# An attention layer and a quantised feed-forward layer on one core: chunk work re-timed, queries seven steps ahead, down projection in six banks

## What is computed

```python
def xattn(query, key, value, mask, Wq, Wk, Wv, Wo):       # 8 x 128 tokens of 512; 32 query heads, 8 kv heads of 128
    q, k, v = heads(query @ Wq), heads(key @ Wk), heads(value @ Wv)
    q, k = apply_rope(q), apply_rope(k)
    logits = einsum('btkgd,bTkd->bkgtT', q, k) * 0.0884
    logits = where(mask, 30 * tanh(logits / 30), -1e30)
    return einsum('bkgtT,bTkd->btkgd', softmax(logits), v) @ Wo

def ffn(x, w1, w2, w3):                                     # 512 -> 1376 -> 512
    dq1, dq2, dq3 = (nf4_quant_dequant(w) for w in (w1, w2, w3))
    return (silu(x @ dq1.T) * (x @ dq2.T)) @ dq3.T

def nf4_quant_dequant(w):                                   # blocks of 64 values
    absmax = max(abs(block)); n = block / absmax
    return NF4_CODE[searchsorted(bounds, n)] * absmax       # 15 bounds, 16 codes

x = x + xattn(layernorm(x), ctx, ctx, mask, ...)
x = x + ffn(layernorm(x), w1, w2, w3)
```

## Time and profile before

| | us |
|---|---|
| median of 3 runs | 882.83 |
| lowest and highest | 882.04, 887.17 |
| the profiled execution, its time | 888.34 |
| its span, first to last instruction | 886.5 |
| PE busy | 815.5 (92%) |
| DVE busy | 684.7 (77%) |
| POOL busy | 484.2 (55%) |
| ACT busy | 464.8 (52%) |

### The profile page before, as it was taken

The page is one execution under the profiler, slowest core; times in us unless marked ns, Lnnn a source line. Parts: engine busy times, 40 slices in busy tenths (PEclk is TensorE's granted clock), DMA queues, the critical chain, the costliest instruction groups (busy, mean ns, idle before and its releaser), DMA issues.

```text
span 886.5 us, 10685 instructions
## 1 busy us (share of the span) xinstructions
PE 815.5 (92%) x3806; PEld 647.4 (73%) x3806; DVE 684.7 (77%) x745; ACT 464.8 (52%) x571; POOL 484.2 (55%) x270
## 2 busy tenths in 40 slices
PE   6798998899899899998999999989779999996898
PEld 4577886688677677776778777767567788885786
DVE  3886853887988789897989989968789889985220
ACT  5025842664766566637647656544544658576100
POOL 2555055675977669769879779683212134432100
PEclk9999999999999999999999999989989999998899
DMA  9667556233343433433434424214003113111210
GB/s 318 187 189 202 167 137 199 72 84 84 109 111 85 135 84 96 126 85 81 139 83 112 132 66 154 72 36 131 30 1 126 36 48 113 48 56 37 74 60 36
DMA packets 63541, 91.76 MB, mean 104 GB/s; under 512 B 6784, under 2 KB 30464, under 8 KB 63488
## 3 DMA queue, kind: packets, MB, share of 16 engines
q1 hardware_dynamic: 62304, 88.25, 34.5%
q10 hardware_dynamic: 1184, 2.82, 0.9%
HBM read 51.00 MB, written 19.07 MB: 79 GB/s over the span
## 4 chain that ended last, share of the span: by engine, by line
PE 54%; DVE 20%; POOL 10%; issue 7%; DMA 5%; ACT 3%; SPq 1%; DVEq 0%; POOLq 0%; ACTq 0%
PE bank L473 5%; PE bank L475 5%; PE bank L474 5%; POOL qT L1169 4%; PE bank L507 4%; PE bank L509 4%; PE bank L508 4%; PE bank L553 3%; PE avp L581 3%; DVE nfv L908 3%; PE bank L493 3%; PE bank L491 3%; PE bank L492 3%; PE trp L480 3%; DVE nfx L908 3%
## 5 line engine op out<-in xcount | busy, mean ns | idle before, releaser
L1226 POOL TENSOR_TENSOR eb<-eb,maskf 128x512 f32<-128x512 f32 x64 | 106.7, 1667 | 53.8 <-ACT eb L782 53.7
L780 ACT ACTIVATE eb<-bank 128x512 f32<-128x512 f32 x64 | 38.1, 595 | 155.8 <-PE bank L553 155.8
L1169 POOL TENSOR_TENSOR qT<-cs_loop,sw 128x512 f32<-128x512 f32 x58 | 90.7, 1564 | 49.2 <-DMA sw<-cs_loop 47.2
L507 PE MATMUL bank<-woh,ath 128*128 128x512 f32 x256 | 110.0, 430 | 0.0
L491 PE MATMUL bank<-xh,wqh 128*128 128x512 f32 x256 | 106.4, 416 | 0.0
L509 PE MATMUL bank<-woh,atl 128*128 128x512 f32 x256 | 103.1, 403 | 0.0
L508 PE MATMUL bank<-wol,ath 128*128 128x512 f32 x256 | 103.0, 402 | 0.0
L493 PE MATMUL bank<-xh,wql 128*128 128x512 f32 x256 | 101.3, 396 | 0.0
L492 PE MATMUL bank<-xl,wqh 128*128 128x512 f32 x256 | 101.1, 395 | 0.0
L716 ACT ACTIVATE nfq<-nfv,bnd 128x1408 uint8<-128x1408 f32 x60 | 84.9, 1461 | 19.7 <-POOL nfv L1185 19.7
L908 DVE SCALAR_TENSOR_TENSOR nfa<-nfq,nfa 128x1408 f32<-128x1408 uint8 x42 | 88.4, 2104 | 0.8
(11 more groups left out here) (140 smaller groups left out, 1960.9 us busy)
## 6 DMA issues: line engine op xcount, KB each, us to landing
sw<-cs_loop SPq DMA_DIRECT2D x116, 128.0 KB, 2.3
stage<-wq_pieces SPq DMA_DIRECT2D x32, 256.0 KB, 2.9
stage<-wo_pieces SPq DMA_DIRECT2D x32, 256.0 KB, 3.0
stage<-dq_scratch SPq DMA_DIRECT2D x32, 256.0 KB, 3.7
sw<-cs_start SPq DMA_DIRECT2D x44, 128.0 KB, 2.4
ks_scratch<-qT SPq DMA_DIRECT2D x16, 256.0 KB, 2.5
vs_scratch<-vst SPq DMA_DIRECT2D x16, 256.0 KB, 2.6
kcur<-ks_scratch SPq DMA_DIRECT2D x16, 256.0 KB, 2.9
```

What stands on the lines that cost most here:

```text
L507: nc.tensor.matmul(o, ah, wh[:, g, :], start=g == 0, stop=False)
L1169: nc.gpsimd.tensor_tensor(dst, products(ru, slot)[:, 0, :], sw[:, slot, :], ALU.add).then_inc(roped, 1)
L1226: nc.gpsimd.tensor_tensor(part, part, maskf[:, :].rearrange("p (o t) -> p o t", o=1).to_broadcast([128, G, S]), ALU.mult).then_inc(weights ...
```

## The change

Query units run seven steps ahead instead of six; the first seven are done in the start phase, and weight pieces are split one step earlier, `high(32)` and `low(32)` ahead of the loop. In the loop every step has exactly two places of NF4 work; the next chunk's maximum stands behind ten additions of the chunk (before: twelve), in the step's own order. POOL divides at the head of the step after that. The loop's last four steps have none of it; the hidden layer has 50 places in 22 units (before: 44), the down projection's first five tiles have 9 additions, behind `w3l` in each tile (before: 3, in two tiles, ahead of it). The chunks of w1 and w2 come in turn, so that the hidden layer starts after fewer of them. Masks of chunks 9 to 11 have a ring of five buffers of their own (`nfz`). The down projection adds up six sequences at a time, two follow.

```diff
-        AHEAD = 6
+        AHEAD = 7
...
-            return {8: 0, 10: 1, 12: 2, 13: 3, 14: 4, 15: 5}.get(v)
+            return {7: 0, 9: 1, 11: 2, 12: 3, 13: 4, 14: 5, 15: 6}.get(v)
...
         def nf_before(slot):
-            if slot <= 56:
-                return max(0, slot - 2) * 116 // 54
             if slot <= NSTEP:
-                return 116 + (0, 1, 2, 3, 4, 6, 8, 10, 12)[slot - 56]
-            return min(128 + 2 * (slot - NSTEP), 16 * 11)
+                return 2 * min(max(0, slot - 2), 58)
+            if slot <= NSTEP + 2 * HT:
+                return 116 + 50 * (slot - NSTEP) // (2 * HT)
+            return min(166 + 2 * (slot - NSTEP - 2 * HT), 16 * 11)
...
-            return [(1 + p // 16, p % 16 - p % 16 // 13) for p in at if p % 16 != 12]
+            return [(1 + p // 16, p % 16 - p % 16 // 11) for p in at if p % 16 != 10]
...
-            return [c for c in range(2, 12) if nf_before(slot) <= 16 * c - 20 < nf_before(slot + 1)]
+            return [c for c in range(2, 12) if nf_before(slot) <= 16 * c - 22 < nf_before(slot + 1)]
...
 SP, in a step of the loop
-                    head_piece(j + 3)
+                    head_piece(j + 4)
...
-                    for c in nf_finished(j - 2):
+                    for c in nf_finished(j - 1):
                         nf_store(c)
-                    for c in nf_finished(j - 3):
+                    for c in nf_finished(j - 2):
...
                     if last and b == 3:
-                        sp.wait_ge(nf_out, nf_stored(NKV - 1))
+                        sp.wait_ge(nf_out, nf_stored(2))
...
 PE, down projection
-            outs = [prj[0], prj[1], prj2[0], prj2[1]]
+            outs = [prj[0][:, :], prj[1][:, :], prj2[0][:, :], prj2[1][:, :], avp[:, 0, :], avp[:, 1, :]]
...
-                for b in range(4):
-                    last = down(b, n, outs[b][:, :])
+                for b in range(6):
+                    last = down(b, n, outs[b])
...
-            for b in range(4, B):
-                pe.wait_ge(final_done, b - 3)
+            for b in range(6, B):
+                pe.wait_ge(final_done, b - 5)
...
 ACT
-                    if not last:
-                        high(32 + j)
+                    if j + 1 < 8 * NKV - 8:
+                        high(33 + j)
...
             weights(0)
+            high(32)
             weights(1)
...
 DVE, down projection
-                if 1 <= n < 3:
-                    for c, i in nf_adds(NSTEP + 2 * HT + n - 1):
-                        nf_add(c, i)
                 nc.vector.tensor_tensor(w3l[0:p, n, :].rearrange("h (a r q) -> h a q r", a=2, q=2),
...
+                for c, i in nf_adds(NSTEP + 2 * HT + n):
+                    nf_add(c, i)
...
 POOL
             for u in range(AHEAD):
-                if u == 5:
+                if u == AHEAD - 1:
                     mask(0)
                 query_rope(u)
...
             mask(1)
+            nf_normalise(1)
+            weight_low(32)
...
+                    for c in nf_prepares(j - 1):
+                        nf_normalise(c)
                     for c in nf_finished(j - 1):
                         nf_rescale(c)
...
                     if j + AHEAD < NUNIT:
                         query_rope(j + AHEAD)
-                    for c in nf_prepares(j) if j else (1,):
-                        nf_normalise(c)
...
-            nf_rescale(NKV)
```

More of the change, by code:

```diff
@@ L132, in build @@
             cs_start = sb("cs_start", [128, 2, 2, 512], f32, start)
+        with ExitStack() as ffn:
+            nfz = sb("nfz", [128, 5, CH], u8, ffn)
         wol1 = sb("wol1", [128, G, D], f32r)
@@ L434, in _ @@
             sp.dma_start(vcur[:, 4:8, 0:DH], vs_d[0, 1]).then_inc(v_in[1], 16)
-            for p in range(3):
+            for p in range(4):
                 head_piece(p)
@@ L438, in _, with w3_in @@
                 head(kv)
[L439 to L449, removed]
             w3v = dq3[:, 0:4 * HID].rearrange("p (i h) -> p i h", i=4)
-            for n in range(HT):
+            def w3_in(n):
                 m = 2 * HT + n
                 cols = 128 if n < HT - 1 else HLAST
-                if n in (2, 7):
-                    nf_store(NKV + 2 + n // 7)
                 if n in (2, 5, 8):
@@ L460, in _ @@
                              w3v[:, :, n * 128:n * 128 + cols]).then_inc(piece_in[m % 4], 16)
+            for n in range(4, 6):
+                weights_in(n)
+            for n in range(2 * HT):
+                if n % 2 == 0 and n + 6 < 2 * HT:
+                    last_column = (n // 2 + 4) * D - 1
+                    sp.wait_ge(nf_out, nf_stored(2 * (last_column // CH) + 2))
+                    weights_in(n + 6)
+                    weights_in(n + 7)
+                for c in nf_finished(NSTEP + n - 1):
+                    if c < NKV + 2:
+                        nf_store(c)
+                for c in nf_finished(NSTEP + n - 2):
+                    if c < NKV + 2:
+                        nf_load(c + 2)
+            for n in range(4):
+                w3_in(n)
+            nf_store(NKV + 2)
+            for n in range(4, 8):
+                w3_in(n)
+            nf_store(NKV + 3)
+            for n in range(8, HT):
+                w3_in(n)
             for b in range(B):
@@ L697, in _ @@
                     w3_transposes(n + 2)
-            for b in range(4, B):
-                pe.wait_ge(final_done, b - 3)
+            for b in range(6, B):
+                pe.wait_ge(final_done, b - 5)
                 for n in range(HT):
-                    last = down(b, n, outs[b - 4][:, :])
+                    last = down(b, n, outs[b - 6])
                 last.then_inc(down_done, 1)
@@ L869, in _ @@
                     .then_inc(wt_hi, 1)
+                for c, i in nf_signs(NSTEP + 2 * HT + n):
+                    nf_above_bound(c, i)
         @block.vector
@@ L1235, in _ @@
                     for n in (28 + u - 1, 29 + u - 1):
[L1236 removed]
+                        weight_low(n)
                 if u == 3:
@@ L1243, in head @@
                 for b in range(B):
-                    j, slot = 8 * kv + b, b % 4
+                    j = 8 * kv + b
+                    for c in nf_prepares(j - 1):
+                        nf_normalise(c)
                     for c in nf_finished(j - 1):
                         nf_rescale(c)
-                    if not last and b < 4:
-                        low(slot, flat(wqh[:, slot, :, :]), flat(wql[:, slot, :, :]), 32 + j)
-                    elif not last:
-                        low(slot, woh[(kv + 1) % 2][:, slot, :], wol[(kv + 1) % 2][:, slot, :], 32 + j)
+                    if j + 1 < 8 * NKV - 8:
+                        weight_low(33 + j)
                     if j + 2 < NSTEP:
@@ L1299 @@
     third = [by_row[:, :, (c + [43])[:11]].reshape(128, CH) for c in cols]
-    nf = np.concatenate([third[0]] + parts + third[1:], axis=1)
+    quarters = [w[:, q * CH:(q + 1) * CH] for q in range(4) for w in parts]
+    nf = np.concatenate([third[0]] + quarters + third[1:], axis=1)
     mask = f(np.asarray(mask_1x1xSxS2_bk0)[0, 0].T)
```

31 lines of the change are left out of this document (17 added, 14 removed).

## The result

The changed kernel takes 857.88 us (median of 4 runs, 855.72 to 859.14) against 882.46 (4 runs, 882.04 to 887.17): a ratio of 0.9707 over all runs, with a 95% interval of 0.9667 to 0.9747 (the two medians alone give 0.9721). Its profiled execution has a span of 853.9 us and a time of 855.72, the fastest of its four.

A forecast was written before the change was run, and what follows sets the result against it. PE was taken as the bound, at 92% busy, with 27.5 us of loop stalls above its floor. Terms summed to -30.1 from the profiled 888.3, giving 858.2, or 852.7 from the median; it took 855, range 846 to 868.

The forecast's parts named there:

- Loop: Steps 3 to 59: ACT's stall behind POOL's dividing goes, and all excess above the step floor with it, -27.5 us.
- The steps with three additions: Main loop: at 1.6 us more these steps took DVE above 8 us; they go with the change.
- Steps 57 to 59: Step 57 loses its query unit, -2.0 us; two DVE additions instead of one give back about 0.9.
- Start: Steps 0 to 2: the extra query unit delays weight pieces, tanh and low part; step 3 starts at 169.5, +5.2 us.
- End of the loop: Steps 60 to 63 without additions shorten DVE's chain to `nrm`; -3.0 us including 0.9 given back in steps 57 to 59.
- Hidden layer: Added additions and a maximum need 13.1 us of DVE, all its 12.9 idle; +3.0 us, bounds 0 and +12.
- DVE becomes the bound: Rival, hidden layer: DVE sets the pace and some loop chunk changes still stall; 862 to 870 us, chance 0.20.
- Down projection: Second wait and the half clock behind it go, first wait grows slightly; -5.8 us, bounds -7 to -2.
- the first wait: Down projection: PE's 5.68 us wait grows by about 0.5 with three DVE additions instead of two.
- The second wait: Down projection: PE's 4.22 us wait goes, as comparisons and additions now stand behind the next high and low parts.
- The port decides: Rival, loop: POOL holds up DVE additions through shared ports, DVE's step becomes 9.0 us; 924 us, chance 0.03.
- The stall only moves: Rival: POOL's dividing delays low part and mask, half of the 27.5 stays, start is dear; about 872 us, chance 0.07.

The follow-up runs named there:

- e10_max_behind_twelve: Changed kernel with the chunk maximum back behind twelve additions instead of ten for the loop's chunks: 871.96 us.
- e12_three_addition_steps: Changed kernel with the old uneven rate in the loop, 116 places in 54 steps, and no additions in steps 56 to 63: 855.72 us.
- e9_low_before_dividing: Changed kernel with early weight pieces, last hidden unit's additions behind the first low part, and POOL's chunk 1 dividing behind the third mask: 844.30 us.
- e6_low_part_first: Changed kernel with the last hidden unit's three additions moved behind the first low part of the third weight: 853.31 us.
- e3_four_banks: Changed kernel with the down projection back in four banks instead of six: 860.64 us.
- e4_w1_then_w2: Changed kernel with w1's four chunks loaded before w2's, and waits for the chunks that a tile needs: 858.07 us.
- e11_divide_at_end: Changed kernel with POOL's dividing back at the end of the maximum's own step, behind the query rope: 858.49 us.

## Why the prediction was right, point by point

*Loop.* Forecast -27.5 to the end of step 59, measured 26.7 to step 57: the chain read from the earlier trace rows is the one that went, and `e10_max_behind_twelve` brings it back. The text gave the lead and the place of the maximum together; alone the lead and the whole chunk schedule are worth 16.6 and 23.6. One link is narrower than the text has it: ACT does not reach the comparison "a step later than POOL ends" but 0.6 us later (212.88 and 213.46). The steps with three additions, which the prediction named as a stall of their own, cost 2.15 us in all (`e12_three_addition_steps`).

*Steps 57 to 59.* Forecast -2.0 for the query unit and +0.9 for DVE's second addition. Measured -0.8 in all (19.20 against 20.03), where 1.3 of the 20.03 was a wait for a query rope that the prediction counts in the loop's excess. DVE with two additions is busy 18.79 of 19.20, and PE waits for `nrm` in each step. Without additions the three steps take 16.36 (`e12_three_addition_steps`), so a step without a query unit needs 5.45 us and not the 5.76 that was called a floor, and DVE's additions cost 2.8 where 0.9 was forecast: this term was too small by a factor of three.

*Start.* Forecast +5.2, measured +2.7 in the profiled execution. The links were as written: the piece, tanh, PE's 5.83, the dividing ahead of the low part. The seven kernels with this start reach step 3 between 167.00 and 170.88, mean 168.9, so +4.6 is the better number, as far as the one profile of the kernel before allows: the profile shown is the earliest of them. The half clock behind these waits lasts 6.8 us in some and 13.7 in others. The links were tested by taking them away: early pieces -5.0, low part before dividing -4.0. What the prediction's lower bound of +2.5 overlooked is that the start of the kernel before had a stall of its own, PE behind POOL's query rope:

```profile
158.49 1.75 PE L553 MATMUL bank<-qT,kcur 128*128 128x512 f32 x2 [3.78 <-POOL qT L1169]
```

It is gone in all kernels with the new schedule. So with the seventh unit and no stall left step 3 starts at 160.88 (`e9_low_before_dividing`), 3.4 us before the old kernel's, and with early pieces alone at 163.44, 0.9 before it.

*End of the loop.* Forecast -3.0 with the +0.9 for steps 57 to 59 in it, so -3.9 from step 60 on; measured -5.5 there. PE's wait in step 61 fell from 5.91 to 2.18, where 2.3 of 5.91 had been taken off. DVE's chain from `nrm` of step 60 to that of step 61 took 11.5 us and takes 7.8: in it lay the two additions, slower than the 3.35 us of two undisturbed ones, and the small `corr`, which takes 0.16 in the changed kernel (timeline, DVE, before).

```profile
630.93 4.25 DVE L908 SCALAR_TENSOR_TENSOR nfv<-nfq,nfv 128x1408 f32<-128x1408 uint8 x2
...
638.28 1.22 DVE L967 TENSOR_TENSOR corr<-guess 128x2 f32<-128x2 f32 x1 [0.83 <-POOL guess L1181]
```

In exchange DVE waits 1.38 for ACT's `ath`, as the prediction had it. Behind the shorter wait PE ran less long at the half clock, 6.8 us instead of 10.2 in this stretch.

*Hidden layer.* Forecast +3.0 for a DVE that has no time left. Measured -0.2 within it. DVE's work grew by 7.7 us (105.14 to 112.88 of 117.79) and not by 13.1, so 4.9 us of idle time were left, and PE never waited for `hf`, though DVE handed over as late as 0.3 us before PE wanted it (in the kernel before, as late as 0.15). The rival that DVE becomes the bound did not come true there. The load was real, though, and came out one stage later.

*Down projection.* Here is the step that failed. The text had the first wait grow "by about 0.5"; it grew by 4.3, from 5.68 to 10.02. The term took DVE to be on time at the end of the hidden layer, while another term of the same sum had it full. DVE came out of the last chunk change 2.5 us later than before (`hf` ended 3.9 instead of 1.4 us behind PE), as much as the two additions beside the rescaling took more (6.00 instead of 3.35). The other 1.8 came with the third addition: 6.42 us for three instead of 3.35 for two, less a wait of 1.2 for ACT's comparisons that DVE no longer had. `e6_low_part_first` takes the three additions off and the wait is 4.97; that the rescaling is what made DVE late is read from the trace, no run moves it away. The second wait went as forecast, the last chunk was in time, and the stage came to -2.1 instead of -5.8. With the hidden layer it is -2.3 against -2.8, so the sum hardly noticed.

*Sum.* -32.6 between the spans against -30.1. From the median 882.46 the gain is 24.6, since the profiled execution of before was 5.9 above its median and that of after 2.2 below. The prediction left 858.2 and 852.7 open, by whether this excess would go with the stalls, and took 855; measured is 857.88, near the first. That the excess sat in stalls of this kind is not shown, since there is one profile of the kernel before. And the closeness is in part luck, for the terms missed in both directions: the down projection gained 3.7 less than forecast and steps 3 to 59 together 1.1 less, while the hidden layer came out 3.2, the start 2.5 and the end of the loop 1.6 better.

*Rivals.* "The port decides" is refuted: the loop's steps never leave 7.74. That DVE additions are slower beside POOL shows in the trace again (two took 6.00 beside POOL's 3.93 and take 3.35 elsewhere, so 2.65 more, less than POOL's operation is long), and it cost PE something only where DVE had no slack. "The stall only moves" did not come true in the loop, where PE has no wait left; at the start it did: POOL's dividing ahead of the low part made PE wait 1.23 in the changed kernel, 2.57 once the pieces were early.

## What to carry to other kernels

When an in-order engine waits at the head of a periodic job for a slow helper, look at the order of issue, not at the helper's speed: a schedule with one step more between the helper's input and the first use took 23.6 us off the loop, while the helper ran as late as before; that step alone, taken back, put all of ACT's waits back. A deeper lead hides the same stall on the bounding engine but has to be paid for where the pipeline fills; with the cause gone it won 3.15 us in the loop and 2.65 behind it, cost 5.7 up to step 3 in the profiles, and lost 4.7 by the medians. And when two terms of a sum share an engine, carry its backlog from the one stage into the next.

## What the runs showed of the hardware beyond that

PE's wait for tanh before the third logits was followed by 6.8 us at 1.2 GHz in the five executions in which it lasted 5.8 to 6.8 us (the changed kernel, `e3_four_banks`, `e4_w1_then_w2`, `e6_low_part_first`, `e12_three_addition_steps`), and by 13.7 us in the two in which it lasted 7.2 (`e10_max_behind_twelve`, `e11_divide_at_end`). The same first three steps took 30.1 to 31.1 us in the five and 32.9 and 33.1 in the two. PE's waits of 0.5 to 1.3 us in steps 57 to 60 had no such spell. DVE and POOL together stayed busy for whole steps (7.72 and 7.75 of 7.75 from 213.44 on in the changed kernel) without PE losing anything.

```profile
213.44:221.19 7.75, 7.75 (x40) 6.18 (x39) 7.72 (x9) 4.96 (x7) 7.75 (x4) 1.00 0.17 52
```
